# A ViT tower block on one Trainium2 core: two of six tokenizer records as rounded halves, one set of four banks, and the class token's steps one group later

## The reference

```
xb   = 2*pi * x[..., None] * freq_bands            # 576 x 6 per token
feat = concat([sin(xb), cos(xb)], -1)              # 6912 per token
h    = feat @ W.T                                  # 192 per token
h    = concat([cls_tok, h])                        # token 0 of each image
h    = h + attn(layernorm(h))                      # gated linear attention, heads normed, @ Wo
h    = h + ffn(layernorm(h))                       # softmax router, 2 of 8 experts, plus a shared expert
```

## Time and profile before

| | |
|---|---|
| median of 3 runs | 557.06 us (554.62 to 557.3) |
| the profiled execution | 554.62 us, of which the span of instructions 552.8 us |
| PE busy | 535.8 us (97%) |
| DVE, ACT, POOL busy | 370.3, 244.4, 180.3 us |
| tokenizer products (L1369) | 289.4 us of PE |
| DMA | 42.49 MB, mean 77 GB/s |

### The profile page before, as it was taken

One profiled execution on the slowest core, in us unless ns is written; L12 is line 12 of the kernel. 1 busy time (PEld: TensorE's weight loads), 2 busy tenths in 40 slices (PEclk: granted clock), 3 DMA queues, 4 the chain that ended last, 5 costly groups with the idle time before them and its releaser, 6 DMA issues.

```text
span 552.8 us, 9034 instructions
## 1 busy us (share of the span) xinstructions
PE 535.8 (97%) x3235; PEld 504.8 (91%) x3235; DVE 370.3 (67%) x1065; ACT 244.4 (44%) x343; POOL 180.3 (33%) x205
## 2 busy tenths in 40 slices
PE   5999999999999999999999999999999999999997
PEld 5998999899999899999989999978877899999865
DVE  8637787534868637978853995468998256666437
ACT  3465464755324764243565422264142135555410
POOL 6413134122234311765212460002601414444510
PEclk9999999999999999999999999999999999999999
DMA  8900067000000001110000010510103441531174
GB/s 330 341 23 20 7 219 250 20 10 20 20 19 21 20 0 27 62 59 0 1 1 10 20 59 1 185 54 30 50 0 125 157 136 47 171 99 51 52 216 142
DMA packets 23488, 42.49 MB, mean 77 GB/s; under 512 B 2502, under 2 KB 15044, under 8 KB 23348
## 3 DMA queue, kind: packets, MB, share of 16 engines
q1 hardware_dynamic: 19560, 33.31, 18.4%
q0 software_dynamic: 3472, 8.07, 4.1%
q10 hardware_dynamic: 412, 0.53, 0.4%
HBM read 31.74 MB, written 14.79 MB: 84 GB/s over the span
## 4 chain that ended last, share of the span: by engine, by line
PE 80%; DVE 11%; ACT 4%; issue 2%; DMA 1%; ACTq 0%; DVEq 0%
PE ps L1369 44%; PE ps L1571 3%; PE ps L1624 2%; PE ps L1626 2%; PE ps L1533 1%; PE ps L1602 1%; PE ps L1603 1%; PE ps L1604 1%; PE ps L1606 1%; PE ps L1605 1%; DMA r<-r 1%; PE ps L1537 1%; PE ps L1535 1%; PE ps L1536 1%; PE ps L1534 1%
## 5 line engine op out<-in xcount | busy, mean ns | idle before, releaser
L1369 PE MATMUL ps<-w_tok,feat 128*128 128x192 f32 x1728 | 289.4, 328 | 7.5 <-ACT feat L502 6.2
L1369 PEld LDWEIGHTS ps<-w_tok,feat 128*128 128x128 f32 x1728 | 282.9, 191 | 8.7 <-issue 8.7
L426 POOL TENSOR_SCALAR feat<-fx 128x512 int32<-128x512 f32 x108 | 93.4, 880 | 189.4 <-PE ps L1369 185.8
L511 ACT ACTIVATE feat<-feat 128x1536 f32<-128x1536 f32 x35 | 52.0, 1485 | 110.1 <-DVE feat L805 110.1
L801 DVE SCALAR_TENSOR_TENSOR feat<-fx,feat 128x512 f32<-128x512 f32 x105 | 76.5, 781 | 1.8 <-POOL feat L426 1.5
L462 POOL DMA_INDIRECT ydram<-yr,xs x39 | 37.8, 969 | 53.9 <-DVE yr L1127 53.9
L514 ACT ACTIVATE feat<-feat,half_pi 128x1536 f32<-128x1536 f32 x35 | 54.6, 1561 | 0.0
L456 POOL DMA_INDIRECT slots<-pay_a,posi x17 | 17.4, 1025 | 75.2 <-DVE posi L1053 71.8
L805 DVE TENSOR_SCALAR feat<-feat 128x1536 int32<-128x1536 int32 x35 | 37.3, 1066 | 1.2
L1571 PE MATMUL ps<-w_down,hid_ring 128*128 128x192 f32 x192 | 35.4, 328 | 2.2 <-DVE H L1085 2.2
L616 ACT ACTIVATE s_ring<-ps 128x512 f32<-128x512 f32 x24 | 14.4, 599 | 52.4 <-PE ps L1537 52.4
(11 more groups left out here) (306 smaller groups left out, 859.6 us busy)
## 6 DMA issues: line engine op xcount, KB each, us to landing
slots<-in_blank SPq DMA_DIRECT2D x1, 5031.0 KB, 19.2
w_tok<-in_wT SPq DMA_DIRECT2D x7, 576.0 KB, 8.9
fx<-in_xT SPq DMA_DIRECT2D x15, 256.0 KB, 2.7
xs<-slots SPq DMA_DIRECT2D x5, 645.0 KB, 5.8
yin<-ydram SPq DMA_DIRECT2D x8, 384.0 KB, 6.6
raw_a<-in_wea SPq DMA_DIRECT2D x4, 384.0 KB, 5.4
raw_b<-in_web SPq DMA_DIRECT2D x4, 384.0 KB, 6.0
w_tok<-in_wT SPq DMA_DIRECT2D x4, 288.0 KB, 7.5
```

The lines of the kernel that those rows point to most:

```text
L426: ins = pool.tensor_scalar(feat[:, k % SLOTS, i, :].bitcast(I32), x[:, x_block(k), :], f_col[:, fi:fi + 1], 1.0, ALU.mult, ALU.mult)
L511: act.activation(feat[:, k % SLOTS, 0:3, :], feat[:, k % SLOTS, 0:3, :], ACT.Sin, scale=TWO_PI).then_inc(sin_ready, 1)
L1369: ins = pe.matmul(ps[:, TOK[a % 2][t // 2], (t % 2) * D:(t % 2 + 1) * D], feat[:, k % SLOTS, i, t * P:(t + 1) * P], w_tok[:, k, i, :], sta ...
```

## The change

1. **Zeros' products at first.** PE multiplies eight 192-column products of zeros (`run_in`) as soon as DVE has cleared the operand, into a bank that is not yet in use. Group 1 of image 0 gets its first sine by itself (`second_remainders`).
2. **Rounded halves.** In groups 1 to 7 of images 1 to 3 (21 groups) records 4 and 5 are multiplied as fp32r halves: one product of 384 columns (high feature x low and high weight) and one of 192 (low feature x high weight) replace one fp32 product of 192. ACT rounds the two features (`feature_high`), DVE makes the remainder in place (`feature_low`), both once per group. The weights are halved once, in image 0 (`weight_high` on ACT, `weight_low` on POOL).
3. **One set of four banks.** Tile t of every image is summed in bank t: columns 192 to 383 the sum, columns 0 to 191 what high feature x low weight gives. In groups 0 and 8 the tiles are the outer loop, `take_h` copies tile by tile, the next image's group 0 waits for these copies, and for images 1 to 3 there are two copies for a tile and DVE adds them (`h_sum`).
4. **Absolute values** of images 1 to 3 go from DVE (L805) to ACT.
5. **Class token a group later.** In image 0 every step from `attn3(0)` stands one group later, and the class token's router comes behind group 8.
6. **Heads not divided.** `attn5` takes the statistics of the undivided heads from PSUM, and adds 1e-5 times the square of the denominator where 1e-5 was added; the reciprocal and the four products with it go.
7. **Halved routers** on PE: images' routers are issued in two halves, the first inside group 0.
8. On ACT, image b's router exponential stands behind group 3's sines, the gate's logarithm ahead of group 4's. The second copy of the last 64 normed columns moves to ACT for images 1 to 3 (`twice`). One `down` step stands behind one more transpose at the start of the routed tiles. The descriptor scratch of POOL's DMAs is 8192 bytes.

The diff, cut to its core:

```
-TOK = ((0, 1), (2, 3))
+TOK = (0, 1, 2, 3)
...
+        def halved(a, k, i):
+            return a >= 1 and 1 <= k <= NG3 and i >= 6 - R3
...
+            def weight_low(k):          # POOL, 128x384
+                pool.wait_ge(whi_ready, k)
+                pool.wait_ge(tok_group, k + 1)
+                pool.tensor_tensor(...).then_inc(wlo_ready, 1)
...
                 elif 0 in halves:
                     act.wait_ge(r_ready, q + 1)
+                    if a >= 1:
+                        act.activation(feat[:, k % SLOTS, 3:6, :], feat[:, k % SLOTS, 0:3, :],
+                                       ACT.Abs).then_inc(abs_ready, 1)
...
+            def feature_high(a, k):
...
+                act.wait_ge(sin_ready, 2 * (NG * a + k) + 2)
+                act.activation(f_hi[:, k % 2, :, :].rearrange("p i t -> p (i t)"),
+                               feat[:, k % SLOTS, 6 - R3:6, :].rearrange("p i t -> p (i t)"),
+                               ACT.Copy).then_inc(fhi_ready, 1)
             def take_h(b):
...
+                for t in range(NT):
+                    if t < NT - 1:
+                        act.wait_ge(tok_tile, (NT - 1) * b + t + 1)
+                    else:
+                        act.wait_ge(tok_group, NG * (b + 1))
+                    ins = act.activation(H[:, b, t, :], ps[:, TOK[t], D:2 * D], ACT.Copy)
+                    if b >= 1:
+                        ins = act.activation(xn[:, t, :], ps[:, TOK[t], 0:D], ACT.Copy)
+                    ins.then_inc(h_tile if t < NT - 1 else h_ready, 1)
...
+            def feature_low(a, k):
+                dve.wait_ge(fhi_ready, halves_before(a, k) + 1)
+                dve.tensor_tensor(f_lo[:, k % SLOTS, 6 - R3:6, :]...,
...
+                if a >= 1 and 2 <= k <= NG3 + 1:
+                    feature_low(a, k - 1)
...
+                    if a >= 2:
+                        dve.tensor_tensor(H[:, a - 1, :, :], H[:, a - 1, :, :], xn[:, :, :], ALU.add).then_inc(h_sum, 1)
...
             split_piece(0)
+            remainders(0, 7)
             attn7(0)
-            remainders(0, 7)
             split_piece(1)
+            remainders(0, 8)
             attn8(0)
...
+            def run_in():
+                pe.wait_ge(blank_ready, 1)
+                for _ in range(RUN_IN):
+                    pe.matmul(ps[:, A0, 0:D], pay_a[1][:, NT, 0:P], pay_a[1][:, NT, 0:D], start=True, stop=True)
+            def record(a, k, i, t):
+                tokens = slice(t * P, (t + 1) * P)
+                out_ = ps[:, TOK[t], D:2 * D]
+                if halved(a, k, i):
+                    f = f_hi[:, k % 2, i - 6 + R3, tokens]
+                    pe.matmul(ps[:, TOK[t], 0:2 * D], f, w_r[:, w_at(k) + i:w_at(k) + i + R3 + 1:R3, :], start=False,
+                              stop=False, skip_group_check=True)
+                    return pe.matmul(out_, f_lo[:, k % SLOTS, i, tokens], w_r[:, w_at(k) + i + R3, :], start=False,
+                                     stop=False, skip_group_check=True)
...
+                if q >= 1 and k in (0, NG - 1):
+                    pe.wait_ge(sin_ready, 2 * q + 2)
+                    for t in range(NT):
+                        if k == 0 and 0 in recs and t < NT - 1:
+                            pe.wait_ge(h_tile, (NT - 1) * (a - 1) + t + 1)
+                        if k == 0 and 0 in recs and t == NT - 1:
+                            pe.wait_ge(h_ready, a)
+                        for i in recs:
+                            ins = record(a, k, i, t)
...
-    nc = bacc.Bacc("TRN2", target_bir_lowering=False, num_devices=1)
+    nc = bacc.Bacc("TRN2", target_bir_lowering=False, num_devices=1, dynamic_dma_scratch_size=8192)
```

More of the change, by code:

```diff
@@ L31 @@
 SLOTS = 3
+NG3 = NG - 2
+R3 = 2
 CLS = 2
@@ L467, in _ @@
                     rounds(b, k)
+                    if b == 0 and k > SLOTS:
+                        weight_low(k - SLOTS)
+                    if b == 1 and k < 2:
+                        weight_low(NG - SLOTS + k)
                     if b >= 2:
@@ L588, in attn6, with twice @@
                                scale=gb_a[:, 0:1]).then_inc(nta_ready, 1)
+            def twice(a):
+                act.wait_ge(xn2_ready, a + 1)
+                act.activation(payload(a)[:, :, D:XD], payload(a)[:, :, P:D], ACT.Copy).then_inc(twice_ready, 1)
             def attn8(a):
@@ L592, in attn8 @@
                 xh_a_, _, xh_b_, _ = operands(a)
+                if 1 <= a < B:
+                    twice(a)
                 act.wait_ge(xpose3, a + 1)
@@ L758, in _, with layernorm @@
         def _(dve):
-            def layernorm(src, dst, a, which, TP, nt, done, twice=False, parts=(0, 1, 2)):
+            def layernorm(src, dst, a, which, TP, nt, done, over=None, parts=(0, 1, 2)):
                 n0 = (3 * a + which) * LNS
@@ L770, in layernorm @@
                     for i in range(nt):
-                        ins = dve.bn_stats(st[0:TP, i, :], src[0:TP, i, 0:D])
+                        ins = dve.bn_stats(st[0:TP, i, :], src(i))
+                    if over is not None:
+                        for lo, d in over:
+                            n = d.shape[1]
+                            ins = dve.tensor_scalar(den[0:TP, lo:lo + n], d, DEN_EPS, None, ALU.add)
                     next_(ins)
@@ L774, in layernorm @@
                         ins = dve.bn_aggr(mv[0:TP, i, :], st[0:TP, i, :])
+                    if over is not None:
+                        ins = dve.scalar_tensor_tensor(den2[0:TP, 0:nt], den[0:TP, 0:nt], LN_EPS, den[0:TP, 0:nt],
+                                                       ALU.mult, ALU.mult)
                     next_(ins)
@@ L777, in layernorm @@
                 if 1 in parts:
-                    next_(dve.tensor_scalar(v_, mv[0:TP, 0:nt, 1], LN_EPS, None, ALU.add))
+                    if over is None:
+                        next_(dve.tensor_scalar(v_, mv[0:TP, 0:nt, 1], LN_EPS, None, ALU.add))
+                    else:
+                        next_(dve.tensor_tensor(v_, mv[0:TP, 0:nt, 1], den2[0:TP, 0:nt], ALU.add))
                     next_(dve.tensor_scalar(y_.bitcast(I32), v_.bitcast(I32), 1, None, ALU.logical_shift_right))
@@ L943, in norm_rest @@
                     dve.wait_ge(scat, scattered(a - 2))
-                layernorm(residual(a), payload(a), a, 2, TP, nt, xn2_ready, twice=True, parts=parts)
+                layernorm(tiles_of(residual(a), TP), payload(a), a, 2, TP, nt, xn2_ready, parts=parts)
+                if 2 in parts and a in (0, B):
+                    for i in range(nt):
+                        ins = dve.tensor_scalar(payload(a)[:, i, D:XD], residual(a)[0:TP, i, P:D], mv[0:TP, i, 0:1],
+                                                y[0:TP, i:i + 1], ALU.subtract, ALU.mult)
+                    ins.then_inc(twice_ready, 1)
             def attn8(a):
@@ L1193, in _ @@
             first_remainders()
-            remainders(0, 1)
+            second_remainders()
             attn0(0)
@@ L1207, in _ @@
             remainders(0, 3)
+            remainders(0, 4)
             attn2(0)
-            remainders(0, 4)
+            remainders(0, 5)
             attn3(0)
@@ L1494, in attn8, with router @@
                 ins.then_inc(xpose3, 1)
-            def router(a):
+            def router(a, half):
                 W, TP, nt = width(a)
                 xh_a_, xl_a_, xh_b_, xl_b_ = operands(a)
-                pe.wait_ge(xh_ready, a + 1)
-                pe.wait_ge(xl_ready, a + 1)
-                if a >= 1:
-                    pe.wait_ge(dz_ready, a)
-                for i in range(nt):
+                if half == 0:
+                    pe.wait_ge(xh_ready, a + 1)
+                    pe.wait_ge(xl_ready, a + 1)
+                    if a >= 1:
+                        pe.wait_ge(dz_ready, a)
+                for i in range(half * nt // 2, (half + 1) * nt // 2):
                     o, c = ps[0:TP, logit_bank(a), 16 * i:16 * i + NR], slice(i * P, i * P + TP)
@@ L1729, in _ @@
                 if q == Q_LG:
-                    router(B)
+                    router(B, 0)
                 if q == Q_RK:
@@ L1734, in _ @@
                     down(q - 2)
+                if q == Q_LG:
+                    router(B, 1)
                 if q == Q_SCORES:
```

231 lines of the change are left out of this document (145 added, 86 removed).

## The result

| | before | after |
|---|---|---|
| median of five runs (lowest to highest), us | 557.06 (554.62 to 557.3) | 560.57 (559.61 to 560.9) |
| span of the profiled execution, us | 552.8 | 558.7 |
| its mean granted clock | 1.000 | 0.994 |

The ratio is 1.0067, 95% interval 1.0043 to 1.0091. The forecast was 555.0, range 548 to 561: the time lies inside the range, but it was expected on the other side of no change, and close to the end that the range had for another reason (an ACT that becomes the bound).

What follows compares the result with a forecast made beforehand. PE was taken as the bound: number of steps times length, plus waits. Image 0 +5.1, halves -6.7, key DMA -0.5, states +0.8, last image +0.3 and -0.95 gave -1.95 on 557.06: 555 us, range 548 to 561.

Steps and rivals of the forecast that it cites:

- an ACT that becomes the bound: Rival: in images 1 to 3 ACT's queue bounds the attention's chain, +6 us, 561; chance 0.14.
- image 0's waits: Three new PE waits in image 0, 1.3, 3.4 and 4.1 us, taken as +8.8 us.
- one such fall as a rival: Rival: PE's clock falls in the 4.1 us gap before image 1, once more +2.4 us, 557.5; chance 0.14.
- the 4.1 us wait: Third new wait: PE between the class token's router and image 1, for router steps, exponential and tile copy.
- the 3.4 us wait: Second new wait in image 0: PE at group 8, forecast to wait 3.4 us, with the cosine needed too.
- no slower steps follow: Argument against the clock's fall: PE's longest wait for sines, 1.1 us, had no slower steps behind it in the chain.
- The first two waits: Image 0, groups 7 and 8: DVE's splits ahead of the remainders make PE wait 1.3 and 3.4 us.
- on the median 557.06 - 1.95: Sum of -1.95 us put on the median, 2.44 above the profiled execution: 555.1, said as 555.
- Halves: Images 1 to 3: 168 pairs of rounded products each save 0.04 us, 6.7 us in all.
- Start: First two groups, 96 records: zeros' products fill PE's idle time and end the slow steps, gain 2.4 us.
- Key DMA and states: Images 1 to 3: key DMA waits fall by 0.5 us; waits for states add 0.8 us.
- Last image: Norm's wait 0.2 to 0.3 us; heads' norm 0.55 and payload 0.4 saved: -0.95 + 0.3 us.

Runs made afterwards that it cites:

- E4: Changed kernel with 11 products of zeros on PE in each of two long waits, ahead of group 8 and image 1's group 0: 558.65 us.
- E2: Changed kernel with DVE making the remainders of groups 7 and 8 in image 0 before the shared expert's splits: 556.26 us.
- E5: Changed kernel with the class token's router on PE between the two halves of group 8, not behind it: 555.66 us.
- E9: Kernel before the change, with the class token's router on PE behind group 8 of image 0, not ahead of it: 565.34 us, ratio 1.0167.
- E1: Changed kernel with ACT copying the four token tiles before the class token's exponential at the end of image 0: 560.81 us, ratio 1.0083.
- F2: Kernel before the change, with the halved routers alone: median 555.73 us, ratio 0.9982.
- E7: Changed kernel with the edits of E1, E2 and E5, without the eight products of zeros at the start: 551.50 us.
- E10: Changed kernel with the edits of E1, E2 and E5, last image's router whole, last but one down products a step earlier: 548.66 us, ratio 0.9873.
- F4: Changed kernel with the edits of E1, E2 and E5, and the last but one down products a step earlier: 549.57 us, ratio 0.9887.
- F1: Changed kernel with the edits of E1, E2 and E5, but routers of images 1 to 3 whole: median 551.46 us.
- E12: E10 plus, in image 0, first records of groups 8 and 0 waiting for sines alone, ACT's tile copies between sines and cosines: 549.10 us.
- F3: F1 with the first half of each router of images 1 to 3 worked out three times: median 562.93 us.

## Why the prediction was wrong

**The failed step: image 0's waits were priced as time and not as idleness of PE.** The sum had +8.8 for them; they were 10.4, and behind the two longest the clock fell, 3.4 us more. I had one such fall as a rival with 14 in 100, priced at 2.4 for the 4.1 us wait. A fall costs 1.7 and it came twice, since the 3.4 us wait (measured 3.97) was not asked the same question. The step "no slower steps follow" argued from a wait of 1.1 us, the longest that the trace had. E4 shows the falls to be due to the waits, as the Trainium skill, TensorE: Matmul & The Clock Gate, Part 1, has it for idleness. That 560.57 lies inside 548 to 561 was luck: the upper end stood for an ACT that becomes the bound, which it did not.

**The size of the waits.** The order was read rightly: DVE's splits stood ahead of remainders (E2), the class token's chain had lost its cover (E5, E9). The first two waits are 0.7 and 0.6 us over the forecast. DVE's lines after (start us, us) say where:

```profile
61.68 1.27 DVE L1218 TENSOR_TENSOR wb<-raw_sb,wb 64x768 fp32r<-64x768 f32 x1
62.98 2.39 DVE L910 SCALAR_TENSOR_TENSOR feat<-fx,feat 128x512 f32<-128x512 f32 x3
65.40 0.96 DVE L917 TENSOR_SCALAR feat<-feat 128x1536 int32<-128x1536 int32 x1
```

I had taken 0.95 us for each half of the split and 2.06 for the three remainders; the second half took 1.27 and the remainders 2.39. Two groups later the remainders took 2.99, while POOL's `rounds` ran all along (81.58 to 84.90), and 2.05 at 93.70, with POOL idle. That POOL's work stretches DVE's fits these three, but no run tested it.

**The third wait, a chain with a second end.** I named DVE's router steps, the exponential and the copy. The steps took 3.7 us (forecast 3.4) and the wait was 4.28. That DVE's own norm of image 1 lies behind the same steps, and that it would hold PE just as long if the copy did not, I did not see; E1 does. For the forecast it made no difference, for the remedy it was all.

**The halved routers had no term.** They cost 0.55 us in the last image and take away the slower level of the times; on the kernel before alone 1.3 us on the median (F2). With it goes the step "on the median 557.06 - 1.95": the 2.44 us between the profiled execution and the median are not an offset that every kernel has but, as far as F2 and E9 show, mostly clock falls of a kind that this change takes away. Against a full-clock execution of before (554.6) the changed kernel is 6 us slower, not 3.5.

**Halves**: forecast -6.7, measured -7.1 by group length. The 192-column step, for which there was no row, is 0.09 us and not 0.11, the 384-column one 0.20 and not 0.174; the sum came out right (0.20 + 0.09 against 0.174 + 0.11) because the two errors cancel, which is luck. **Start**: -2.4 against -2.1, of which the zeros give 1.5 in E7's executions; the early sine shows no gain. Nearly right. **Key DMA and states**: -0.5 and +0.8 against -0.65 and +1.2, right in place. **ACT in images 1 to 3**: 306 us busy, not the bound; that rival fell. The 27 absolute values took 1.48 us each there, and no table load comes with them (29 in all, 33 before). The rounding of 1024 columns was put at 0.83 times 1.25, where 1024/768 is 1.33; it took 1.06 us, and nothing hung on it. **Last image**: forecast -0.65, measured +1.0. The heads' norm wait (0.55) did go, but the next wait on DVE grew from 0.61 to 1.45, so the saving was given back one step later; the ranks' 0.54 and 0.22 more at the tile are the halved router and the moved down products (E10, F4).

In one line: -1.95 became +5.95 by clock 3.4, waits of image 0 1.7, last image 1.65 and 1.15 of small terms, of which image 0's rest of 0.7 is the largest.

## What to carry to other kernels

Where PE is the bound, ask of every new wait and of every long row of tiny products whether the clock falls behind it; one fall here costs what the rounded halves save in five groups (1.7 against 0.34 each). Before undoing a wait, follow the chain behind it to its second meeting with PE: the edit that pays is the one at the chain's start. And before forecasting from one profile, look whether the runs lie on two levels, and which level the profile is of.

## What the runs showed of the hardware

- A fall takes the granted clock to 0.50 for some 3.4 us, once for twice as long (E9), and 3.4 us of it cost 1.7 us of fp32 products. After the start it followed each of the eight waits of PE of 3.8 us or more in the profiled executions, one of the four of 2.03 us (E4), and none of those of 1.65 us.
- 20 products of ten columns in 2.24 us, with PE busy by its records all the time, can be followed by a fall just the same, in some executions and not in others (E9, F1, E12); 40 in 4.5 us were each time in the profiled execution (F3). With the rows cut into two of ten and other products between, 5 of 37 runs and none of F2's 12 were at a mean clock under 0.998.
- Without products ahead of them PE's first 9 to 17 fp32 records stand 0.32 us apart, later ones 0.16 (before, E7, F2). With 16 records of zeros ahead at most one did. How many differs between executions.
- A product of 192 fp32r columns behind one of 384 takes 0.09 us from start to start, less than the 0.11 us of a ten-column one in a row of its like.
